# Six shared columns in 22 groups of 286 nodes, half as many slot tiles, and slots that belong to one column

## The reference

```python
in_agg = segment_sum(edge_feat, dst-side index, 6250)    # by one end of each edge
out_agg = segment_sum(edge_feat, src-side index, 6250)   # by the other end
h = relu(concat([in_agg, out_agg, x]) @ W1 + b1)         # 192 -> 256
x = layernorm(x + h @ W2 + b2)                           # 256 -> 64
```

## Time and profile before

| | |
|---|---|
| median of three runs | 1434.71 us (1432.44 to 1435.06) |
| the profiled execution | 1431.8 us; its span, first to last instruction, 1430.0 us |
| early chunks and ranks | 0 to 99.4 us |
| 78 sharing chunks | 99.4 to 787.8 us |
| 18 summing chunks | 787.8 to 1349 us |
| dense layers | 1349 to 1430 us |
| mean granted TensorE clock | 0.984 of full speed |

### The profile page before, as it was taken

The page is one execution under the profiler, slowest core; times in us unless marked ns, Lnnn a source line. Parts: engine busy times, 40 slices in busy tenths (PEclk is TensorE's granted clock), DMA queues, the critical chain, the costliest instruction groups (busy, mean ns, idle before and its releaser), DMA issues.

```text
span 1430.0 us, 63740 instructions
## 1 busy us (share of the span) xinstructions
PE 1345.7 (94%) x23675; PEld 1055.1 (74%) x23675; DVE 1350.9 (94%) x3463; ACT 1009.2 (71%) x2185; POOL 1154.9 (81%) x663
## 2 busy tenths in 40 slices
PE   3559999999999999999999899999999999999896
PEld 2349999999999999999999566566666666566543
DVE  6989999999999999999999999999999999998586
ACT  6528888878888888888778666766776667676443
POOL 3888888888888888888888888888888888888633
PEclk9969999999999999999999999999999999999998
DMA  9327777787777777778888777777767777767541
GB/s 300 46 16 191 191 190 190 191 190 193 196 196 196 194 193 193 196 197 219 218 216 219 186 188 196 185 183 186 181 171 186 187 181 208 166 155 181 97 134 43
DMA packets 216557, 255.41 MB, mean 179 GB/s; under 512 B 99251, under 2 KB 179220, under 8 KB 216214
## 3 DMA queue, kind: packets, MB, share of 16 engines
q1 hardware_dynamic: 123880, 223.88, 49.1%
q0 software_dynamic: 92384, 28.77, 22.4%
q10 hardware_dynamic: 144, 0.67, 0.2%
HBM read 143.18 MB, written 110.08 MB: 177 GB/s over the span
## 4 chain that ended last, share of the span: by engine, by line
PE 51%; DMA 17%; POOL 15%; issue 10%; DVE 6%; ACT 0%; DVEq 0%; POOLq 0%; SPq 0%; ACTq 0%
PE psum L1580 21%; PE psum L1603 19%; DMA out_tables<-payload,target 16%; POOL out_tables L711 15%; PE psum L1557 3%; PE psum L1564 2%; PE psum L1643 1%; PE psum L1776 1%; PE psum L1641 1%; PE psum L1767 1%; PE psum L1788 1%; DMA rows_i<-in_dst 1%; DVE from_group L1072 1%; DVE same L1260 1%; DVE in_group L1109 1%
## 5 line engine op out<-in xcount | busy, mean ns | idle before, releaser
L711 POOL DMA_INDIRECT out_tables<-payload,target x628 | 1121.5, 1786 | 209.7 <-issue 186.3
L1580 PE MATMUL psum<-parts,to_slot 128*128 128x194 bf16 x6552 | 587.2, 248 | 0.2 <-ACT slots_out L806 0.2
L1580 PEld LDWEIGHTS psum<-parts,to_slot 128*128 128x128 bf16 x6552 | 553.7, 98 | 16.3 <-issue 0.4
L1603 PE MATMUL psum<-to_node,slots_in 64*64 64x448 bf16 x9828 | 480.8, 351 | 4.8 <-DVE to_node L1233 4.0
L1603 PEld LDWEIGHTS psum<-to_node,slots_in 64*64 64x64 bf16 x9828 | 283.7, 107 | 180.0 <-issue 5.6
L806 ACT ACTIVATE slots_out<-psum 128x388 bf16<-128x388 f32 (+1 forms) x936 | 366.4, 472 | 55.3 <-PE psum L1580 47.2
L1194 DVE TENSOR_SCALAR to_slot<-iota_h,slot 128x896 bf16<-128x896 f16 x936 | 381.9, 460 | 0.1
L1233 DVE TENSOR_SCALAR to_node<-iota_h,slot_rel 128x448 bf16<-128x448 f16 x819 | 268.6, 346 | 0.8 <-PE psum L1603 0.5
L1233 DVE TENSOR_SCALAR to_node<-iota_rows,slot_rel 128x448 bf16<-128x448 f16 x546 | 236.7, 434 | 0.0
L867 ACT ACTIVATE to_node<-apart 128x448 bf16<-128x448 bf16 x273 | 149.0, 573 | 67.2 <-PE psum L1603 66.5
L830 ACT ACTIVATE payload<-psum 128x256 f32<-128x256 f32 x157 | 60.2, 383 | 180.3 <-PE psum L1643 176.3
(11 more groups left out here) (127 smaller groups left out, 771.6 us busy)
## 6 DMA issues: line engine op xcount, KB each, us to landing
slot_tiles<-slots_out SPq DMA_DIRECT2D x78, 1018.5 KB
feat<-in_edge_attr SPq DMA_DIRECT2D x195, 256.0 KB
slots_in<-slot_tiles SPq DMA_DIRECT2D x40, 970.0 KB
slots_in<-slot_tiles SPq DMA_DIRECT2D x40, 921.5 KB
out_tables<-payload,target POOLq DMA_INDIRECT x628
out_tables<-zeros POOLq DMA_DIRECT2D x4, 1600.0 KB
feat<-out_tables SPq DMA_DIRECT2D x48, 128.0 KB, 2.2
slots_in<-slot_tiles SPq DMA_DIRECT2D x14, 242.5 KB
```

Source lines behind the costliest of these rows:

```text
L711: e.indirect_dma_start(out_tab, at, payload[b][:, t, :], None, element_offset=k * TABLE_ROWS * D, compute_op=ALU.add).then_inc(s_tab[k], 16)
L1580: last = e.matmul(ps_share[r % BANKS][:, o:o + SLOT_W], to_slot[m][:, k, g * P:(g + 1) * P], parts[b][:, SHARE_FROM + MINI * m + k, 1:], s ...
L1603: return e.matmul(ps_groups[g % 2][h][cols, 0:HOT], slots_in[p % RING][rows, j - PART_FROM[p], D * k:D * (k + 1)], to_node[rows, node_buf( ...
```

## The change

The changed kernel has a batch of six columns and two batches a chunk, 22 groups of 286 nodes (11 pairs). A group's 64 slots are no longer open to every column: each of six columns has 8 of its own ("home" slots) and 16 are shared by what is past the eighth. The home slots of the six columns lie one column after another, `22 x 8 = 176` for each, and the shared ones behind them. So a column needs only the tiles with its home slots and those with shared ones: `to_slot` has 640 slots for a column (768 for one of six) in place of 896, and a batch has 31 products, a chunk 62, in place of 84. A chunk writes 2 x 11 = 22 tiles instead of 21, in runs of two tiles (776 bytes) instead of three (1164 bytes). Now 4 chunks are early, 82 share and 12 sum; 1804 tiles are summed, each against 286 nodes instead of 448. The scatters are 580: 64 early, 328 in the sharing chunks, 188 after.

```diff
-FIRST = 2
-MINIS = 3
-MINI = 4
+FIRST = 4
+MINIS = 2
+MINI = 6
-GROUP_NODES = 448
+GROUP_NODES = 286
+HOMES = (8,) * MINI
+SHARED = SLOTS - sum(HOMES)
+HOME_AT = [SLOT_GROUPS * sum(HOMES[:k]) for k in range(MINI + 1)]
+    COLUMN_TILES.append(together + list(range(SHARED_TILE, NODE_PAIRS)))
-HOT_ROW = 64
-SUMS = 18
+HOT_ROW = 26
+SUMS = 12
-PARTS = 3 * RING
+PARTS = 2 * RING
-PIECES = 4
+PIECES = 2
...
+            def load_tiles(g, p, a, z):
+                lo = PART_FROM[p]
+                homes = slot_rows[0:HOME_AT[MINI], :].rearrange("(k r) w -> k r w", k=MINI)
+                for h in range(2):
+                    into = slots_in[p % RING][SLOTS * h:SLOTS * (h + 1), a - lo:z - lo, :].rearrange("p t w -> p (t w)")
+                    group = 2 * g + h
+                    e.dma_start(into[0:SLOTS - SHARED, :],
+                                homes[:, HOMES[0] * group:HOMES[0] * (group + 1), a * SLOT_W:z * SLOT_W]).then_inc(s_slot_in[p % RING], 16)
+                    at = HOME_AT[MINI] + SHARED * group
+                    e.dma_start(into[SLOTS - SHARED:, :], slot_rows[at:at + SHARED, a * SLOT_W:z * SLOT_W]
+                                ).then_inc(s_slot_in[p % RING], 16)
             def load_part(g, p):
-                e.dma_start(slots_in[p % RING][:, 0:hi - lo, :].rearrange("p t w -> p (t w)"),
-                            slot_tab[bass.ds(g, 1), :, lo * SLOT_W:hi * SLOT_W].rearrange("g p w -> p (g w)")
-                            ).then_inc(s_slot_in[p % RING], 16)
+                load_tiles(g, p, *PART_FROM[p:p + 2])
...
             def ranks():        # TensorE
-                    for j, (a, w) in enumerate(RANK_PIECES):
-                        e.matmul(bank[4 + j][:, 0:w], above_bf[:, :], flat[:, a:a + w], start=True, stop=False)
+                    for k in range(MINI):
+                        for g in range(SLOT_GROUPS):
+                            last = e.matmul(ps_counts[:, k, g, :], in_group[:, k, g, :], ones_bf[:, 0:2], start=True, stop=True)
                     for g in range(SLOT_GROUPS):
+                        last = e.matmul(ps_group, ident_bf[:, :], from_group[:, :, g, :], start=(g == 0), stop=(g == SLOT_GROUPS - 1))
+                    e.wait_ge(s_pre, PRE_EARLIER[n])
+                    for k in range(MINI):
+                        for a, (g, w) in enumerate(RANK_BANKS):
+                            turn = len(RANK_BANKS) * (MINI * n + k) + a
+                            if turn >= len(RANK_BANKS):
+                                e.wait_ge(s_first, turn - len(RANK_BANKS) + 1)
+                            for j in range(w):
+                                last = e.matmul(to, above_bf[:, :], in_group[:, k, g + j, :], start=True, stop=(k == 0))
+                                if k > 0:
+                                    last = e.matmul(to, earlier_bf[0:BATCH_TILES, k, g + j:g + j + 1].to_broadcast([BATCH_TILES, P]),
+                                                    ident_64[0:BATCH_TILES, 0:BATCH_TILES], start=False, stop=True)
+                    e.wait_ge(s_masked, MINI * (n + 1))
+                    for g in range(SLOT_GROUPS):
+                        last = e.matmul(ps_found, ident_h[:, :], place[:, :, g, :], start=(g == 0), stop=(g == SLOT_GROUPS - 1))
...
             def slot_round(s, b, r):
-                    for k in range(MINI):
-                        last = e.matmul(ps_share[r % BANKS][:, o:o + SLOT_W], to_slot[m][:, k, g * P:(g + 1) * P],
-                                        parts[b][:, SHARE_FROM + MINI * m + k, 1:], start=(k == 0), stop=(k == MINI - 1))
+                    columns = TILE_COLUMNS[g]
+                    for k, t in columns:
+                        last = e.matmul(ps_share[r % BANKS][:, o:o + SLOT_W], to_slot[m][:, COLUMN_FROM[k] + t * P:COLUMN_FROM[k] + (t + 1) * P],
+                                        parts[b][:, SHARE_FROM + MINI * m + k, 1:], start=((k, t) == columns[0]),
+                                        stop=((k, t) == columns[-1]))
```

More of the change, by code:

```diff
@@ L28 @@
+import struct
 from contextlib import ExitStack, contextmanager
@@ L242, in build @@
             with ExitStack() as sharing:
-                to_slot = [sharing.enter_context(nc.sbuf_tensor(f"to_slot{m}", [P, MINI, SLOT_COLS], bf16)) for m in range(MINIS)]
+                to_slot = [sharing.enter_context(nc.sbuf_tensor(f"to_slot{m}", [P, COLUMN_FROM[MINI]], bf16)) for m in range(MINIS)]
                 slots_out = [sharing.enter_context(nc.sbuf_tensor(f"slots_out{b}", [P, NODE_PAIRS, MINIS, SLOT_W], bf16))
@@ L841, in chunk @@
                         put_sums(before, q - 2, c)
[L842 removed]
+                    if ahead and not first_sums and q == 0:
                         split_mid(c + 1, 1 - b)
[L844 to L852 removed]
             def to_far(g, i):
[L854 removed]
+                p, n = part_of(i), scalar_rounds(tile_no(g, i)) - 1
                 e.wait_ge(s_slot_rel, g * PARTS + p + 1)
@@ L881, in tiles_to_nodes @@
                         flush(ends[part - 1] // TILES - 1)
[L882 removed]
+                    mine = [divmod(n, TILES) for n in range(cuts[part], min(cuts[part + 1], ALL_TILES)) if by_scalar(n)]
                     for k in range(0, len(mine), APARTS):
@@ L1104, in nodes_of, with surplus_of @@
                 step(last)
+            def surplus_of(n):
+                e.wait_ge(s_counts, n + 1)
+                last = e.tensor_scalar(surplus[0:BATCH_TILES, :, :], ps_counts[:, :, :, 0], float(HOMES[0]), 0.0,
+                                       ALU.subtract, ALU.max)
+                step(last)
+                step(e.tensor_copy(earlier[0:BATCH_TILES, 1, :], surplus[0:BATCH_TILES, 0, :]))
+                for k in range(1, MINI):
+                    step(e.tensor_tensor(earlier[0:BATCH_TILES, k + 1, :], earlier[0:BATCH_TILES, k, :], surplus[0:BATCH_TILES, k, :],
+                                         ALU.add))
+                e.tensor_reduce(fullest[0:BATCH_TILES, n:n + 1], earlier[0:BATCH_TILES, MINI, :], AX.X, ALU.max)
+                step(e.tensor_copy(earlier_bf[0:BATCH_TILES, 1:MINI, :], earlier[0:BATCH_TILES, 1:MINI, :]))
+                assert steps[0] == PRE_EARLIER[n], (n, steps)
@@ L1106, in ranks @@
             def ranks():
                 for n in range(BATCHES_OF_RANKS):
-                    step(in_groups(n, range(11 if n == 0 else 1, SLOT_GROUPS)))
                     step(e.tensor_tensor(in_group[:, :, :, :], from_group[:, :, 0:SLOT_GROUPS, :], from_group[:, :, 1:, :],
                                          ALU.subtract))
-                    for k in range(MINI - 1):
-                        step(e.tensor_tensor(before[:, k + 1, :, :], before[:, k, :, :], in_group[:, k, :, :], ALU.add))
@@ L1113, in ranks @@
-                    if n > 0:
-                        e.wait_ge(s_totals, n)
-                    step(e.tensor_tensor(counts[:, :, :], before[:, MINI - 1, :, :], in_group[:, MINI - 1, :, :], ALU.add))
                     assert steps[0] == PRE_GROUPS[n], (n, steps)
@@ L1685, in chunk @@
                         payload_quad(c, b, d, mode, q)
-                    if mode.window and not is_final(c) and q == QUADS - 1:
+                    if mode.window and not is_final(c) and c != FIRST - 1 and q == QUADS - 1:
                         spread(c + 1, 0, mode.n)
```

327 lines of the change are left out of this document (171 added, 156 removed).

## The result

The changed kernel took 1772.2 us (median of four runs, 1752.3 to 1787.5) against 1434.8 before: a ratio of 1.231 (1.221 to 1.241), slower. Forecast was slower, at 1624 in a range to 1720: the sign was right, the size was not. The profiled execution has a span of 1767.1 us. Medians in this document are of all runs of a kernel and ratios of its fast ones alone, which parts the two for `one_halves`: two of its four runs, the profiled one among them, were in a slower state, and the two fast ones took 1539.4 and 1556.7 us.

A forecast was written before the change was run, and what follows sets the result against it. PE and DVE, both 94% busy, were taken as the bound before, six-engine home loads in summing after. 213 + 690 + 638 + 79 = 1620 us span, 1624 with run overhead; range 1490 to 1720, slower.

The forecast's parts named there:

- The bounds of the kernel before: PE and DVE both bound it at 94% busy; a sharing chunk's chain of waits is PE alone, 8.79 us.
- the engines alone: Summing: by DVE, PE and POOL work without transfers the stage falls from 561 to 460 us.
- Step 1, ranks: Early chunks and ranks: two batches of 54 us each, so sharing starts at 213 us instead of 99.4; range 195 to 235.
- The 242 rank products: Ranks, per batch: 242 products of 82 columns on PE at .075 us each, so 18 us.
- Step 2, sharing: 82 sharing chunks at 8.25 us, plus 14 where first home pieces are read: 690 us, ends 650 and 725.
- hides below that: Sharing: DMA's 7.1 to 8.8 us a chunk hides below the chunk length taken as 8.2 us.
- Step 3, summing: Summing: home loads on six DMA engines set the pace, 638 us instead of 561; six engines' chance .83.
- the 90 for scatters: Summing: 188 scatters at .478 us on every DMA engine add 90 us.
- The Trainium skill's rule: Loads use the largest number up to 16 dividing both sides' slowest dimension; 6 against 48 gives 6 engines.
- That the loads spread anyway: Rival in summing: loads use 16 engines, DVE sets the pace, summing 464, kernel 1423 us, faster; chance .08.
- That POOL holds the chunk at 8.6: Rival in sharing: loads spread, but POOL keeps the chunk at 8.6; kernel 1465 us, slower; chance .06.
- The Trainium skill's rule on the shared port: DVE's two-port fast operations hold GpSimd's port for a whole instruction; had it alone decided, sharing chunks would stay at 8.6.

The follow-up runs named there:

- one_halves: one_load with slot sums written in runs of 1552 B, half after each chunk, SP waiting for that chunk's sums: 1560.7 us, ratio 1.045.
- one_plain: one_load, but each load takes 128 neighbouring table rows (wrong out_agg, time only): 1531 us, ratio 1.034.
- flat_plain: Changed kernel with slot writes of one 8536-byte run a partition and parts read as 128 neighbouring rows (wrong out_agg): 1466.6 us, ratio .989.
- before_388: Kernel before with a chunk's slot sums written by three DMAs in runs of 388 bytes instead of one in runs of 1164: 1554 us, ratio 1.051.
- flat_writes: Changed kernel with a chunk's slot sums written as one 8536-byte run a partition instead of eleven of 776 (wrong out_agg): 1644.5 us, ratio 1.146.
- one_wide: one_load with slot sums of two chunks written by one DMA in runs of 1552 bytes: 1684 us, ratio 1.138.
- after_again: Changed kernel once more, no edit, on a chip of the second group: 1716 us, ratio 1.156.
- one_load: Changed kernel with shared slots numbered in two blocks of 176, so a part is one DMA of 16 rows by eight blocks: 1612 us, ratio 1.088.
- before_six: Kernel before with each half of a part read as in the changed kernel, 48 rows in six blocks plus 16 rows: 1603.6 us, ratio 1.115.
- homes8: Changed kernel with home loads read as eight rows by six blocks instead of six blocks by eight rows: 1672 us, ratio 1.131.
- homes16: Changed kernel with each part read by eight DMAs of 16 rows instead of two of 48 and two of 16: 1593 us, ratio 1.113.
- before_apart: Kernel before with a part read as 16 rows by eight blocks 16 rows apart (wrong out_agg): 1519 us, ratio 1.027.
- apart_one: one_load with pairs of groups g and g + 11, slots numbered by rank first, a pair's rows 11 apart: 1639 us, ratio 1.105.

## Why the prediction failed, step by step

**The bounds of the kernel before** were read rightly in sharing: without the transfers' cost a chunk takes 8.09 us (forecast 8.2) where PE needed 8.79. In summing the engines alone were put at 460 us; with cheap transfers one_plain and flat_plain take 495 and 501. DVE's 441 us of work was right (444.6 in flat_plain, from 884 to 1390), but the waits among the engines are some 60 and not 20.

**Step 1, ranks:** right, 18 us too long. `in_group` took 5.79 (5.9), the 22 group sums 6.2 (6.5). The 242 rank products are the term that was mis-sized: .04 us each where I took .075 from products of 117 columns; they took 10.5 us a batch, at the pace of ACT's copies, not 18. A batch took 45 us (from `in_group` at 100.49 to the next at 145.24), not 54.

```profile
115.59 6.36 PE L1585 MATMUL psum<-from_group,ident_bf 128*128 128x492 bf16 x22
121.79 1.27 PE L1595 MATMUL psum<-in_group,above_bf 128*128 128x82 bf16 x23
```

**Step 2, sharing: the step that failed,** 135 us. The sentence was that DMA's 7.1 to 8.8 us a chunk "hides below that", below a chunk of 8.2. Both ends were given, and only the low one hides. The packet records show an engine's time for one chunk, until the first pieces are read: 5.0 us for the main queue and 1.8 for scatters before, 7.0 and 1.8 after, 8.85 in all. The table has the main queue's share of 16 engines over 100 us of sharing, divided by its packets, and then the mean of each kind alone, over all sharing before the first pieces:

| run | mean packet | time of one | packet of the slot write | 2 KB packet of features |
|---|---|---|---|---|
| before_388, 500 to 600 us | 518 B | 53 ns | 388 B: 46 ns | 146 ns |
| after | 953 B | 66 ns | 776 B: 55 ns | 129 ns |
| before | 1313 B | 67 ns | 1164 B: 63 ns | 92 ns |
| one_halves | 1607 B | 80 ns | 1552 B: 82 ns | 85 ns |
| flat_writes | 3830 B | 183 ns | 8536 B: 430 ns | 85 ns |

A write packet with a third fewer bytes saves only 8 of 63 ns, so 57% more write packets cost 42% more engine time (3.5 to 4.9 us a chunk), though bytes grew by 5%; the features beside them cost .6 us more. The share over the stage is .88. What it cost in the profiled run: the common chunk 8.75 instead of 8.25, over 66 chunks 33 us; seven stretches of about 8.2 us and two of 3, some 63; and where the home pieces are read, 185 us for 16 chunks where 146 were forecast. That is the 135. flat_writes removes the first two, and one_halves the first, in the group that has no stretches. one_wide shows that it is not engine time alone: the same long runs in bursts take as little of it (6.7 us a chunk, one_halves 6.8) and left the chunk at 9.8. I had taken DMA for a rate to compare with a period, but the scatters and the features stand in the same engines, and a scatter that lands 4 us late stops ACT. What makes it land late is not settled: after_again and one_load have a share of .90 until the first pieces are read, no chunk over 9.9 us there, and landings of 5 to 8 us where their chains show them.

**Step 3, summing:** right in kind, 29 us short. The loads cost, not the engines: 528 with sixteen engines for the 667 of six. No trace here names the engine of a packet, but the number of slot packets in flight does as well: most often six in after and before_six, eight in homes8, sixteen in before and one_load. That the sum came so near is partly luck. The slot packets moved 20.0 B/ns over the stage where I took 23.6, so 67.2 MB over six engines are 560 us and not 475, and the sum would be 723. Some other term was 56 too high; it may be the 90 for scatters, which no run takes by itself. The Trainium skill's rule ("DMA: Bandwidth & Descriptors", "Why a DMA increments its semaphore by 16 and not by 1") made the forecast possible, and the form of the load put into the kernel before cost 170 us, on the side that the rule says. What neither it nor my sum had is the second cost, below, which the repaired loads met and the changed kernel did not, and SP's issues, which replace the wait when the loads are cut small.

**Rivals.** That the loads spread anyway: refuted by homes16 and by the six packets in flight. Its 1423 us would not have come either: flat_plain, with cheap reads and writes, takes 1466.6. That POOL holds the chunk at 8.6: refuted, since flat_writes leaves POOL's work as it is and the chunk is 8.09. The Trainium skill's rule on the shared port ("SBUF — State Buffer", "SBUF: two separate sides") is borne out by single rows only, here a scatter of 6.41 us beside the 5.79 of `in_group`; it does not set the pace.

```profile
101.37 6.41 POOL L744 DMA_INDIRECT out_tables<-payload,target  x1 [0.31 <-issue]
```

The range was too narrow for the reason that failed step 2: with the high end of the DMA bound as the pace, the chunk would have been 8.8, which is 45 of the 148 us.

## What to carry to other kernels

Count a DMA's packets as well as its bytes, and before counting on "hides below", put the whole range of the engines' time beside the period: an end that lies above it does not hide. The share alone is not a limit: at .80 (flat_writes) the chunk kept DVE's pace, at .90 (after_again) it was .8 us longer, and before_388 shows 1.20 from 100 to 700 us, since the two queues' packets overlap in time. Look at the first count of both sides of a load, and when you repair it, at the distance between the rows: one_load uses sixteen engines and still lost 79 us in summing by the rows it reads. A table whose rows are regrouped to save products must be written and read back, and that is where this change lost. In the second group, where both were run, making both transfers cheap takes the kernel from 1716 to 1467 us, against 1482 for the kernel before: 1% gained by the engines, 17% lost in transfers.

## What the runs showed of the hardware that was not expected

Reads slow down when one DMA gathers rows that are far apart in DRAM. Main queue over 100 us of summing: neighbouring rows for each engine in before and one_plain,

```profile
q1 hardware_dynamic: 3028, 16.16, 47.5%
```
```profile
q1 hardware_dynamic: 3314, 18.85, 54.4%
```

and steps of 176 rows (one_load), 16 rows (before_apart) and 176 rows, with different engines 11 rows apart (apart_one):

```profile
q1 hardware_dynamic: 2750, 16.45, 68.8%
```
```profile
q1 hardware_dynamic: 2880, 15.13, 65.1%
```
```profile
q1 hardware_dynamic: 2343, 14.99, 63.8%
```

That is 34 and 35 MB for 100 us of full share against 24, 23 and 23.5. A row of a part is as long in all of them (7.4 to 8.1 KB). The slot packets alone, over the whole summing stage, moved 21.0 to 22.5 B/ns in before, before_388, one_plain and flat_plain, and 14.3 to 15.0 in one_load, before_apart and apart_one. If a DMA's rows are dealt to the engines by its first count, what those three kernels share is that one engine steps over 1.4 MB or more from row to row within a DMA; that engines read close together is not the cause, since apart_one parts them and is as slow. But the step is not the whole cause. In homes16 sixteen engines read sixteen neighbouring rows, and an engine's next row, in the next DMA, lies 176 rows away again; yet its slot packets moved 19.0 B/ns. before_six, with steps of six rows, has 19.0 too, and after 20.0 with neighbouring ones. Whether the step counts only within one DMA, from how many rows on, and what in DRAM or on the way causes it, stays open; so does a rival that no run excludes, that a source of two levels is itself slower on sixteen engines. Open too is why the kernel before takes 1433 us in one group of runs and 1480 in the other (before_apart has 9.4 us a sharing chunk, the kernel before had 8.8), and why the stretches of 17 us appear in the first group alone, while the mean of the changed kernel's other chunks before the first pieces is 8.8 and 8.9.
